# Graph network on one core: one-hot matrices of layers 2 and 3 made once and streamed, preparation re-ordered

## The reference, cut to what matters

```
L0: 10 rounds of  h = 0.9 * norm * segment_sum((h * norm)[src], dst) + 0.1 * h0
L1: q = h[src] @ Wq;  k, v = h[dst] @ Wk, h[dst] @ Wv;  4-head attention weights exp(clip(q.k)),
    normalised over src;  segment_sum(att * v, src)
L2: h @ Wself.T + b + (segment_sum(h[src] * weight, dst) / degree) @ Wneigh.T + b
L3: segment_sum(sigmoid(edge_attr @ ps_w.T) * (h * cj)[src], dst) * ci
```

## Time and profile before

| | us |
|---|---|
| median of three runs (1238.22 to 1241.88) | 1238.45 |
| the profiled execution, its own time | 1255.07 |
| its span from the first to the last instruction | 1253.3 |
| busy: PE 967.4, DVE 961.5, POOL 662.5, ACT 600.1 | |

### The profile page before, as it was taken

How to read it: one execution, slowest core, us unless ns; L and a number is a source line. 1 busy time by engine, 2 the same in 40 slices (tenths; PEclk the granted TensorE clock), 3 DMA queues, 4 the chain that set the end, 5 groups by cost and what they waited for, 6 DMA issues and landing times.

```text
span 1253.3 us, 32626 instructions
## 1 busy us (share of the span) xinstructions
PE 967.4 (77%) x12003; PEld 732.8 (58%) x12003; DVE 961.5 (77%) x1247; ACT 600.1 (48%) x1503; POOL 662.5 (53%) x446
## 2 busy tenths in 40 slices
PE   4967577887999999999994767877772777727773
PEld 3645456776444544545543667877772777727763
DVE  8887878888565555565446499999998689978996
ACT  5531027777111111111101477878784389838984
POOL 1008888888788888888788889988100000000000
PEclk9977786555999999999995688888896589978998
DMA  8643214555222222222303388777834877728774
GB/s 167 130 104 74 53 28 165 191 191 153 57 71 69 83 70 69 83 70 83 67 2 111 117 275 276 265 270 267 301 137 172 341 289 282 279 83 291 282 299 137
DMA packets 73565, 202.18 MB, mean 161 GB/s; under 512 B 36667, under 2 KB 37467, under 8 KB 73509
## 3 DMA queue, kind: packets, MB, share of 16 engines
q1 hardware_dynamic: 57300, 186.25, 41.3%
q10 hardware_dynamic: 2465, 13.60, 4.8%
q0 software_dynamic: 13744, 1.59, 4.1%
HBM read 155.30 MB, written 45.63 MB: 160 GB/s over the span
## 4 chain that ended last, share of the span: by engine, by line
PE 42%; DVE 34%; issue 15%; DMA 4%; ACT 3%; DVEq 2%; SPq 0%; ACTq 0%
PE ps L1640 24%; DVE arena L982 4%; PE ps L1592 4%; DVE arena L948 4%; DVE arena L936 4%; DVE arena L957 3%; PE ps L1495 2%; DVE arena L1032 2%; PE ps L1452 2%; DVE arena L962 2%; PE ps L1437 2%; DMA base_room<-ohd_table 2%; DVE h_room L962 2%; PE ps L1482 2%; DMA hl_room<-in_edge_attr_dram 2%
## 5 line engine op out<-in xcount | busy, mean ns | idle before, releaser
L561 POOL DMA_INDIRECT w_table<-wpa,slot_i x425 | 657.1, 1546 | 218.3 <-issue 218.3
L1640 PE MATMUL ps<-arena,hl_room 125*128 125x500 f16 (+1 forms) x1750 | 342.7, 352 | 2.6 <-DVE hl_room L1218 2.0
L1437 PE MATMUL ps<-arena 125*128 125x64 f16 (+1 forms) x3900 | 232.0, 211 | 87.4 <-ACT arena L606 52.5
L1640 PEld LDWEIGHTS ps<-arena,hl_room 125*128 125x128 f16 x1750 | 155.7, 97 | 162.6 <-issue 4.6
L1437 PEld LDWEIGHTS ps<-arena 125*128 125x128 bf16 x3900 | 178.8, 103 | 93.4 <-ACT arena L606 50.5
L701 ACT ACTIVATE part_room<-ps 128x500 f16<-128x500 f32 (+1 forms) x70 | 38.0, 543 | 306.6 <-PE ps L1640 247.4
L1227 DVE SCALAR_TENSOR_TENSOR part_room<-ps,part_room 128x500 f16<-128x500 f32 (+1 forms) x70 | 43.6, 622 | 149.2 <-ACT part_room L701 143.6
L1442 PE MATMUL ps<-arena 125*128 (+1 forms) x1300 | 136.1, 205 | 0.0
L606 ACT ACTIVATE arena<-ps 128x384 f32<-128x384 f32 x325 | 130.9, 504 | 7.9 <-PE ps L1442 6.2
L632 ACT ACTIVATE arena<-ps,part_room 128x64 f32<-128x64 f32 x500 | 107.9, 339 | 18.6 <-PE ps L1437 10.9
L1442 PEld LDWEIGHTS ps<-arena 125*128 125x128 bf16 x1300 | 114.7, 108 | 0.5
(11 more groups left out here) (266 smaller groups left out, 1468.6 us busy)
## 6 DMA issues: line engine op xcount, KB each, us to landing
hl_room<-slot_rows SPq DMA_DIRECT2D x49, 832.0 KB, 4.3
arena<-slot_rows SPq DMA_DIRECT2D x38, 832.0 KB, 15.8
arena<-ohd_table SPq DMA_DIRECT2D x26, 832.0 KB, 5.0
arena<-ohs_table SPq DMA_DIRECT2D x25, 832.0 KB
base_room<-ohd_table SPq DMA_DIRECT2D x24, 832.0 KB, 5.9
hl_room<-in_edge_attr_dram ACTq DMA_DIRECT2D x17, 750.0 KB
ohs_table<-xs_room SPq DMA_DIRECT2D x25, 448.0 KB
ohs_table<-xs_room SPq DMA_DIRECT2D x25, 384.0 KB
```

Source lines behind the costliest of these rows:

```text
L561: pool.indirect_dma_start(w_table, bass.IndirectOffsetOnAxis(slot_i[:, u:u + 1], 0), wpa[:, u], None).then_inc(S[f"w_out{g % 2}"], 16)
L1437: last = pe.matmul(ps[:, m % RING, o:o + b - a], slots[:, k * L:(k + 1) * L], rhs, start=(i == 0), stop=(i == 1))
L1640: last = pe.matmul(ps[:, c, 0:w], hl[0:P, u, s, :], adj[:, s, c * CH * P:c * CH * P + w], start=(s == 0), stop=(s == T - 1))
```

## The change

- **Gather one-hots of layers 2 and 3**: no longer made by DVE in each layer. In layer 0 SP broadcasts each half slot row into `turn_row` (in `h_room`; layer 0's node values move to a small `h_new`), DVE turns it into one-hots in place (`gather_one_hots`), and SP stores it in a new `oht_table`, ahead of the `ohs_table` half of the same stage. The 50 halves now go over nine iterations (six or five per iteration), and the DVE loop is written out.
- **Loads in layers 2 and 3**: SP loads the 25 gather one-hot tiles of each layer into four buffers, each three tiles ahead of its gather. The scatter one-hots of the 13 even tiles are kept from layer 2 on, the 12 odd ones are loaded into two buffers.
- **Split of a tile**: PSUM groups of 6, 6, 6 and 8 columns; DVE weights three (18 columns), ACT one (8 columns). Groups 0 and 1 alternate between two banks.
- **Loops** of these layers are written for four tiles at a time, and PE writes out the first 13 steps.
- **Preparation**: the first variance moves from behind the scans to after the flag, the first scale behind the bounds; PE does 3 rather than 7 feature groups ahead of the link matmul; ACT's run sums come earlier; the feature groups go between pairs of sort tiles in portions of 1 or 2 (all 22), where 18 went in portions of 2 or 3 and four after the sort; SP reads the flag before it waits for `edge_place`.

```diff
-        EA_FIRST, EA_RUN, EA_END, EA_FLAG, EA_SORT = 4, 11, 37, 40, 46
-        EA_BETWEEN = (46, 48, 50, 53, 56, 59, 61, 64)
+        EA_FIRST, EA_RUN, EA_SQUARE, EA_END, EA_FLAG, EA_STD, EA_SORT = 4, 7, 10, 37, 40, 43, 46
+        EA_BETWEEN = (46, 48, 50, 52, 53, 55, 57, 58, 60, 62, 64, 66, 68)
-        GROUPS = {"l1": [2] * (C // 2), "l2": [8, 8, 5, 5], "l3": [8, 8, 5, 5]}
-        BY_VEC, BY_ACT = 2, 2
+        GROUPS = {"l1": [2] * (C // 2), "l2": [6, 6, 6, 8], "l3": [6, 6, 6, 8]}
+        BY_VEC, BY_ACT = 3, 1
...
+                def turned(d, q):
+                    sp.dma_start(oht[q], oht_table[bass.ds(d, 1)].rearrange("t p x -> p (t x)")).then_inc(S[f"oht_in{q}"], 16)
...
+                def body(d, q, on):
+                    if 0 in on and not (type(d) is int and d < 4):
+                        sp.wait_ge(S[p + "_gath"], (d - 1) * ng)
+                        turned(d, q)
+                    if 3 in on and q % 2 == 0 and not (type(d) is int and d < 8):
+                        sp.wait_ge(S[p + "_scat"], d - 4)
+                        odd(d - 3, (q + 1) % 4)
...
+                def turn_half(t, half):
+                    sp.wait_ge(S[f"turn_out{half}"], t * 16 + 16)
+                    sp.dma_start(turn_row[:, half], slot_rows[0, bass.ds(t * (C * L) + half * CH2, CH2)].partition_broadcast(L)).then_inc(S[f"turn_in{half}"], 16)
+                def keep_half(t, half):
+                    a = sum(KG[:half]) * OW
+                    sp.wait_ge(S["turn_made"], t * 2 + (half + 1))
+                    sp.dma_start(oht_table[bass.ds(t, 1), :, half * CH2:(half + 1) * CH2].rearrange("t p x -> p (t x)"), turn_row[:, half]
+                                 ).then_inc(S[f"turn_out{half}"], 16)
+                    sp.wait_ge(S["ohs_made"], t * 2 + (half + 1))
+                    sp.dma_start(ohs_table[bass.ds(t, 1), :, a:a + KG[half] * OW].rearrange("t p x -> p (t x)"), ohs_words[half]
                                 ).then_inc(S[f"ohs_out{half}"], 16)
+                turn_half(0, 0)
+                with sp.Fori(0, T - 1) as t:
+                    turn_half(t, 1)
+                    keep_half(t, 0)
+                    turn_half(t + 1, 0)
+                    keep_half(t, 1)
...
+            last_run_sums(0, 7)
+            for g in range(EA_RUN - 1):
                 turned_features(g, g + 1)
-                last_run_sums(5 + 2 * g, 7 + 2 * g)
+                last_run_sums(7 + 3 * g, 10 + 3 * g)
...
-                    if 0 in on:
-                        ohT_of(s, par, 0, pair_no)
                     if 3 in on:
                         vec.wait_ge(S[p + "_high"], s - 2)
...
+                def gather_one_hots(t, half):
+                    vec.wait_ge(S[f"turn_in{half}"], t * 16 + 16)
+                    vec.tensor_scalar(turn_row[:, half], turn_row[:, half], lane[:, :], None, ALU.is_equal).then_inc(S["turn_made"], 1)
...
+                        if (2 * i + u, c) in STAGES:
+                            k = STAGES.index((2 * i + u, c))
+                            gather_one_hots(k // 2, k % 2)
+                            scatter_one_hots(k // 2, k % 2)
+                STAGES = [(it, c) for it in range(K0 - 1) for c in range(NCH) if c != NCH - 2 and (c != 2 or it % 2 == 0)]
```

More of the change, by code:

```diff
@@ L46 @@
 CP = C // 2
+CH2 = CP * L
 TOP_W, TOP_CJ, TOP_N, NTOP = 3, 4, 5, 6
@@ L1260, in two_iterations @@
                         if turn:
-                            new_nodes(i, n)
+                            new_nodes(i, n, not more and u == 1)
                         if more or n + 1 < 2 * NCH:
@@ new lines, in gather1, with gather23 @@
+                    last.then_inc(S["l1_gath"], 1)
+                def gather23(t, q, m, c, n):
+                    if m == 0:
+                        pe.wait_ge(*arrived(p, "oht_in", q, t))
+                    if m >= BY_VEC:
+                        pe.wait_ge(S[p + "_last_rows"], t * BY_ACT + (m - BY_VEC + 1))
+                    elif m >= SPREAD:
+                        pe.wait_ge(S[p + "_rows"], t * BY_VEC + (m + 1))
+                    elif not (type(t) is int and t == 0):
+                        pe.wait_ge(S[p + "_rows"], (t - 1) * BY_VEC + (m + 1))
+                    for k in range(c, c + n):
+                        o = (k - c) * w
+                        for i in range(2):
+                            rhs = parts2[:, k, i, :] if k < T else parts2[:, bass.ds(t, 1), i, :].rearrange("p t f -> p (t f)")
+                            last = pe.matmul(ps[:, bank_of(m, q), o:o + D], oht[q][0:P, k * L:(k + 1) * L], rhs,
+                                             start=(i == 0), stop=(i == 1))
+                    last.then_inc(S[p + "_gath"], 1)
@@ new lines, in scatter23 @@
+                def scatter23(t, q, pair_no):
+                    par = q % 2
+                    if par:
+                        pe.wait_ge(*arrived(p, "odd_in", q, t))
+                        words = odd_ohd[q // 2]
+                    else:
+                        if p == "l2" and type(t) is int and t // 2 in KEPT:
+                            part = kept_part(t // 2)
+                            pe.wait_ge(S[f"kept{part}"], 16 * ((KEPT + [(T + 1) // 2])[part + 1] - t // 2))
+                        words = kept_ohd[:, bass.ds(pair_no, 1)].rearrange("p k (a r b) -> p (k a) r b", a=CP, b=2)
+                    pe.wait_ge(S[p + "_low"], t + 3)
+                    pe.wait_ge(S[p + "_sums"], t + 1)
+                    for k in range(C):
+                        last = pe.matmul(ps[:, RING + par, 0:m1], words[:, k // 2, :, k % 2], msg2[:, par, k, :],
+                                         start=(k == 0), stop=(k == C - 1))
+                    last.then_inc(S[p + "_scat"], 1)
@@ L1653, in _ @@
                 layer2_inputs(2)
+                pe.wait_ge(S["taken_v"], turn(max(g for g, p in enumerate(PLAN) if p[1] == "v")))
                 edge_layer("l2", 2)
```

329 lines of the change are left out of this document (175 added, 154 removed).

## The result

| | before | after |
|---|---|---|
| median, us | 1240.16 (1238.22 to 1243.56, 4 runs) | 1210.13 (1207.15 to 1212.05, 4 runs) |
| profiled execution, us (span) | 1255.07 (1253.3) | 1212.05 (1210.2) |

What follows compares the result with a forecast made beforehand. PE and DVE were taken to bound the kernel, DVE in layers 2 and 3. Preparation -9.5, layer 0 +4.9, layers 2 and 3 -15.3 and -14.8 sum to -34.7: 1204 us, range 1190 to 1222.

Steps and rivals of the forecast that it cites:

- The mechanism in layers 2 and 3: Layers 2 and 3: DVE loses its one-hot operation, ACT and DVE set the pace, tile 3.70 us, sum gained 30.1 us.
- PE keeps its 78 matmuls, 3.2: Layers 2 and 3: PE's work per tile stays at 3.2 us, below the 3.70 of the tile.
- Rival 1: Layers 2 and 3: DMA engines take over the loop, tile 3.94 us at share 0.85, time 1215; chance 0.16.
- The sign of a share of about 0.9 over layer 2: Layer 2: a DMA share of about 0.9 was named as one sign that the forecast is right.
- Layer 0: Layer 0: the added one-hot operation costs 0.54 us in each of nine iterations, 4.9 us lost, bounds 0 and 10.
- Preparation: Before layer 0: link wait, variance and sort together gain 9.5 us, bounds 5 and 16; the sort gives 2.
- The restarts that I deducted for: Sort: smaller portions mean twice as many PE restarts at half clock, so a gain of only 2 us was taken.
- The link wait: Preparation: DVE's idle 6.59 us for the link matmul goes entirely with three groups ahead, at least 4.0.
- Rival 2: Whole kernel: everything hidden, layer 0 loses nothing, the sort gains 6, layers 2 and 3 gain 32, time 1193; chance 0.14.
- Rival 4: Layer 0: DVE waits for gather one-hot rows, 25 us lost, time 1229; chance 0.05 shared with a layer 2 clock fall.
- Rival 3: Layers 0 and 1: new DVE operations block POOL, its table comes late for layer 2, time 1286; chance 0.05.
- The offset of 16.6 us: Whole kernel: the profiled execution stands 16.6 us above the median before, and the same difference was assumed after the change.

Runs made afterwards that it cites:

- e1: The changed kernel with PE's even tiles in the loops of layers 2 and 3 taking scatter weights from a fixed address (wrong weights): 1196.9 us, ratio 0.9668.
- e2: The changed kernel with PE's loop over the last 12 tiles of layers 2 and 3 written out, computation whole: 1201.1 us, ratio 0.9703.
- e8: The changed kernel with the edits of e2 and e3 together, all computed: 1195.8 us, ratio 0.9623.
- e3: The changed kernel with chunk 4's gather one-hots in layer 0 built at chunk 6's stage, behind the new nodes: 1204.7 us, ratio 0.971.
- e7: The changed kernel with PE's link product behind seven more feature groups again, in place of three: 1217.6 us, one run.
- e5: e2 with each gather one-hot load from the fifth tile on cut to its first half (wrong weights for 13 groups): 1194.5 us, one run.
- e6: The changed kernel with the old portions of feature groups (two or three, four behind the last tile) in the sort: 1213.2 us, ratio 0.9763.

## Why the prediction was right, and where it was off

1. *The mechanism in layers 2 and 3: right.* No L936 is left, L1034 is 0.47 us as I took it (1.41 for three), and DVE and ACT share the pace. Where nothing disturbs it, the tile is 3.54 to 3.58, under my 3.70: the 0.1 for ACT's register work was not there, and DVE comes out at 1.41 + 1.88 + 0.26, without the 0.08 that I had added. PE's waits for the loads into `base_room`, 16.7 us in layer 2 before, are gone, as said.
2. *The term that was mis-sized: "PE keeps its 78 matmuls, 3.2".* It keeps them, but 26 of every second tile in the loop got a register address, and took 3.46 us in place of 1.46. That even tile needs 3.46 + 1.53 = 4.99 on PE, so PE, which I had last in the row of engines, sets the pace of a pair: 8.1 in layer 2 where twice 3.54 is 7.1. In the change the ten even steps behind the loops' entries stand 10.6 us over 3.54, the two entries 5.8, in which a stop and the clock share. Taking the register address away gains 9.7 (e1), 10.3 (e2) and 8.4 (e8 against e3), between single profiles; e7's layers 2 and 3, the same as the change's, took 3.1 us more than the change's. A row of before could have told it: under `kept_rows` the register address was on one DVE instruction, L936, with one operation of 80 ns:

```profile
L936 DVEq FUSED_REGOPS  x18: 80/80/86, 1029.9 to 1224.4; - x18
```

Moving the choice of the tile to PE's weights makes it 26. (My 3.14 us from start to start for PE also added the gather's duration of 1.68, where a gather takes 1.52 to the next start; that did no harm, as PE was given room.)

3. *What is left in e2 is code.* e5 against e2: 4.1 + 1.4 = 5.5 us, and e5 has 3.54 to 3.58 in every tile: 92.7 + 93.1 - 2 x 85.0 = 15.8 = 10.3 + 5.5. That is e2's split; in the change itself the addresses weigh more and the code less, as there are fewer stops. The measured 3.86 and 3.88 a tile stand 0.16 and 0.18 over my 3.70, so the two layers gave 21.7 us by the first profile of before and 17.9 by the second, not 30.1 (24 tiles and first gather each).
4. *Rival 1 (DMA) was wrong as put.* The loop held 3.54 at a share of 0.96, over the 0.91 I asked for; PE waited for no `oht_table` load. The sign of a share of about 0.9 over layer 2 did not come as named: it was 0.96 and then 0.66. Full engines did cost, through PE's code, a way I had not named. By the Trainium skill's 358 GB/s (*DMA: Bandwidth & Descriptors*, "Where 436 GB/s comes from") that stretch could not have run above it; it moved 369 over 44 us, so here the measurement decides.
5. *Layer 0: right in size and cause.* Forecast 35.7 an iteration, measured 35.72; e3 moves the operation alone and gets 4.3 us back. Against the two profiles of before, layer 0 is 5.1 or 2.8 us longer in the change, so the forecast of 4.9 is met only within that spread. The operation itself took 0.65 us (median), over my bound of 0.60.
6. *Preparation: too low.* To the placed copy 8.9 or 9.4 us where I counted 7.5; PE's groups 40 to 45 took nothing back. They do stand on the path, in the change too: PE goes from L1632 through them to the transposes L1638 that the placed copy waits for, without idle time.

```profile
81.91 0.59 PE L1632 MATMUL ps<-arena,ones 6*128 6x6 f32 x2 [0.80 <-DVE arena L1162]
...
91.34 1.02 PE L1596 MATMUL ps<-part_room,psw 128*26 128x125 f32 x8
92.29 2.80 PE L1638 MATMUL ps<-ident,arena 85*125 85x85 f32 x15
```

But the matmul ahead of them came at 81.91 where it had come at 90.88, 9.0 us earlier, and all of it arrived. The sort gave 2.8 to 7.1 where I took 2; 4.4 by e6, in which the clock may share. The restarts that I deducted for are not seen: the sort's granted clock is 0.81, over the 0.74 and 0.80 of before. The link wait went entirely, as said, but nearly half of it by an earlier load and a full clock, which I had not foreseen (e7).

7. *Rivals 2 to 4.* Rival 2's 32 us for layers 2 and 3 stands in no sum of mine (it is 30.1); what it asked of layer 0 did not come. Rival 4 did not come either: DVE has no idle time before its new operation in the change. Rival 3 had 0.05, and POOL was not late. POOL wrote 234 columns in layer 0 at 1233 ns each, against 226 at 1246, and read the table back at 864.8, long before 930:

```profile
L627 POOL DMA_INDIRECT w_table<-wpa,slot_i x234 | 288.6, 1233 | 71.3 <-issue 71.3
```

8. *The offset of 16.6 us.* I took it as a constant; it belonged to one execution. The forecast of a difference was not harmed, but differences between single profiles were: 43 us of them for 30 of medians.

So 1204 was 6 us low, 1.7 of them from the median of before: layers 2 and 3 gave 8 to 12 less than forecast, preparation 3 to 7 more. That these two partly cancelled is luck. The pace that I named, DVE and ACT together, held wherever PE's addresses were fixed and its code in time; in the loops over the last 12 tiles PE set it, which the prediction did not allow for.

## What to carry over

When one operand of a group of instructions is moved to a kept buffer, look at how its address is chosen. A register address costs one register operation per instruction that uses it: cheap on one long DVE instruction, and dear on 26 weight loads that come every 56 ns, which then no longer run ahead of the matmuls. Writing the loop out removes it, and pays with code that has to come through the same DMA engines as the data; so look for idle PE marked issue in the middle of a group. And before small stage differences are read from two profiles, take the profile of the old kernel twice.

## What the runs showed of the hardware

- Weight load and matmul pairs of 128 columns run at 56 ns each with fixed addresses and at 124 with a register operation of 46 ns between them. The Trainium skill, *TensorE: Matmul & The Clock Gate*, "Architectural detail: the array is 16× 32×32, not 1× 128×128", says that PE's queue can pull weight loads ahead of matmuls in flight. The trace agrees for fixed addresses, and shows that with a register operation ahead of each load it is gone.
- Code arrives during the run, in packets of 16 KB on the instruction queue: one every 6.3 us in e2's layer 2, some 1.8 tiles of PE's instructions. At a DMA share of 0.84 PE stopped for up to 2.0 us beside them, at 0.65 it did not, up to the last tiles.
- A `tensor_scalar` of 1664 bf16 columns took a median of 0.65 us. The 74 of POOL's columns in layer 0 that overlapped one took 1.28 us on average, the other 159 took 1.21; over all, 1.23, where it was 1.25 before the change. Rival 3 drew on the Trainium skill, *SBUF — State Buffer*, "Who interferes with whom", for a lock of at most 27 us; 0.07 us on 74 columns is 5.2 (an estimate from these means), so a full lock for the whole length is not seen here.
